# MLP products of split parts, and a second-product bank that alternates by group

## The reference, cut to what matters

```
x_norm2 = modulate(_ln(x), shift_m, scale_m)     # per sequence
h = jax.nn.gelu(x_norm2 @ W_mlp1 + b_mlp1)       # 128 -> 512 channels
h = h @ W_mlp2 + b_mlp2                          # 512 -> 128 channels
x = x + gate_m[:, None] * h
```

## Time and profile before the change

| what | value |
|---|---|
| median of three runs | 579.82 us (578.67 to 581.12) |
| profiled execution, its own time | 578.05 us |
| span of that execution (first to last instruction) | 576.3 us |
| mean granted TensorE clock | 0.994 of full |
| TensorE busy | 540.8 us (94%) |
| VectorE, ScalarE, GpSimd busy | 424.9, 385.2, 271.3 us |
| stretch of the MLP's products | 324.2 to 404.95 us |

### The profile page before, as it was taken

How to read it: one execution, slowest core, us unless ns; L and a number is a source line. 1 busy time by engine, 2 the same in 40 slices (tenths; PEclk the granted TensorE clock), 3 DMA queues, 4 the chain that set the end, 5 groups by cost and what they waited for, 6 DMA issues and landing times.

```text
span 576.3 us, 16509 instructions
## 1 busy us (share of the span) xinstructions
PE 540.8 (94%) x6175; PEld 381.4 (66%) x6177; DVE 424.9 (74%) x1255; ACT 385.2 (67%) x897; POOL 271.3 (47%) x294
## 2 busy tenths in 40 slices
PE   7988998998999999999999889988999999999995
PEld 6745665666666666666667544444788788788895
DVE  4688987878899798899787445555586786786565
ACT  6548686777878778787777744564654854854862
POOL 5638669299494878888903110124034034034000
PEclk9999999899999999999999999999999999999998
DMA  4764656254143543334400010000001001000000
GB/s 130 162 173 127 175 155 164 56 122 126 52 116 89 134 115 97 105 90 115 114 5 3 2 36 0 2 1 19 0 19 40 18 20 36 18 18 20 19 20 18
DMA packets 48716, 39.38 MB, mean 68 GB/s; under 512 B 6241, under 2 KB 48002, under 8 KB 48642
## 3 DMA queue, kind: packets, MB, share of 16 engines
q1 hardware_dynamic: 46568, 34.62, 23.1%
q10 hardware_dynamic: 2074, 3.77, 2.3%
HBM read 10.06 MB, written 2.10 MB: 21 GB/s over the span
## 4 chain that ended last, share of the span: by engine, by line
PE 64%; DVE 12%; POOL 7%; DMA 5%; SPq 4%; issue 4%; ACT 3%; ACTq 0%; DVEq 0%; POOLq 0%
PE PS L939 35%; PE PS L1810 6%; PE PS L1776 5%; DVE NM L1592 3%; PE PS L975 3%; PE PS L1862 3%; SPq L1324 3%; PE PS L1874 2%; DMA Qs<-MT 2%; PE PS L1794 2%; PE PS L1832 2%; DMA Ks<-Kp 2%; PE PS L1867 2%; POOL rstd L1370 1%; POOL rest L1401 1%
## 5 line engine op out<-in xcount | busy, mean ns | idle before, releaser
L1592 DVE TENSOR_REDUCE NM<-PS 128x4 f32<-128x512 f32 x256 | 163.3, 681 | 30.8 <-PE PS L1776 30.2
L1478 ACT ACTIVATE PR<-PS 128x512 f32<-128x512 f32 x256 | 140.0, 601 | 27.1 <-PE PS L1794 26.5
L1776 PEld LDWEIGHTS PS<-Ks,Qs 64*128 64x128 bf16 x1024 | 57.0, 94 | 53.9 <-DVE NM L1592 29.3
L1776 PE MATMUL PS<-Ks,Qs 64*128 64x128 bf16 x1024 | 83.2, 218 | 6.4 <-DVE NM L1592 3.7
L1794 PE MATMUL PS<-Qs,Ks 64*128 64x128 bf16 x1024 | 83.6, 218 | 3.8 <-DMA Qs<-MT 3.2
L1810 PE MATMUL PS<-PR,Va 128*32 128x128 f32 x2048 | 82.9, 280 | 0.0
L733 ACT ACTIVATE r_HID<-PS,ANC 128x128 f32<-128x128 f32 x224 | 63.4, 383 | 20.2 <-PE PS L939 20.2
L648 POOL TENSOR_TENSOR m_veps<-m_mv,m_eps 128x4 f32<-128x4 f32 x16 | 3.2, 201 | 143.2 <-DVE m_mv L812 143.2
L1794 PEld LDWEIGHTS PS<-Qs,Ks 64*128 64x128 bf16 x1024 | 57.0, 94 | 7.4 <-DMA Qs<-MT 3.7
L1810 PEld LDWEIGHTS PS<-PR,Va 128*32 128x32 f32 x2048 | 48.3, 109 | 20.2 <-ACT PR L1478 6.1
L939 PE MATMUL PS<-r_NXS,r_WNS 128*128 128x512 f32 x168 | 53.1, 424 | 0.0
(11 more groups left out here) (197 smaller groups left out, 1102.3 us busy)
## 6 DMA issues: line engine op xcount, KB each, us to landing
Qs<-Qp SPq DMA_DIRECT2D x96, 128.0 KB
Ks<-Kp SPq DMA_DIRECT2D x90, 128.0 KB
CTXG<-in_ctx SPq DMA_DIRECT2D x8, 256.0 KB, 3.8
r_CTX<-in_ctx SPq DMA_DIRECT2D x8, 256.0 KB, 2.7
out<-X SPq DMA_DIRECT2D x8, 256.0 KB, 2.3
X<-in_x SPq DMA_DIRECT2D x7, 256.0 KB, 4.4
W<-in_weights ACTq DMA_DIRECT2D x2, 855.0 KB
Qs<-MT SPq DMA_DIRECT2D x62, 8.0 KB
```

Source lines behind the costliest of these rows:

```text
L1478: nc.scalar.activation(PR[:, u, :], T_BANK[u % 2][:, :], ACT.Exp, scale=SCALE)\
L1592: nc.vector.tensor_reduce(out=NM[:, c.b // 2, c.second, u // 2, u % 2 * 4:u % 2 * 4 + 4, 0], in_=S_BANK[score_bank(c, u)[0]][:, :].rearran ...
L1776: last = nc.tensor.matmul(S_BANK[bank][:, j * P:(j + 1) * P], Qs[c.stack][rows, lo + j, cols], Ks[c.stack][rows, lo + j, cols], start=True ...
```

## The change

Both MLP products are computed from split parts. The weights get parts W1S and W2S, written by GpSimd in two more weight splits in round 7 (at places 9.0 and 12.0; the old ones move up in number). m_XT gets parts XTS, two buffers by the parity of the group, written by VectorE in a new step xt_parts: a copy to the high part, then a subtraction. Each chunk of m_H gets parts HS, one buffer: after its gelu ScalarE copies the chunk to the high part, and GpSimd subtracts. Every product becomes three matmuls. xt_read moves to right behind xt, and no longer waits for the firsts of the group before but for its xt_parts.

The second product's bank is PS[3] or PS[4] by parity, and the turn back goes into the same bank. So its first second(g,0) waits for x_added (turn_back of group g-2), not for gate of group g-1. The loop of cycles 3 and 4 is written out, since the parity must be known. Tiles Qs and Ks are placed elsewhere in SBUF, since the new tiles reuse freed room.

```diff
-                 + [(t, "split", "weights", k, 0) for k, t in enumerate((2.5, 6.0, 22.5, 24.5))]
+                 + [(t, "split", "weights", k, 0) for k, t in enumerate((2.5, 6.0, 9.0, 12.0, 22.5, 24.5))]
...
-                 + mlp_steps(8.46, "first", 1, 3) + mlp_steps(8.47, "xt_read", 2) + mlp_steps(8.48, "gelu", 1, 2)
+                 + mlp_steps(8.46, "first", 1, 3) + mlp_steps(8.35, "xt_read", 2) + mlp_steps(8.36, "xt_parts", 2) + mlp_steps(5.11, "xt_parts", 1) + mlp_steps(8.48, "gelu", 1, 2)
...
 MLP_STEPS = (
-    ("stats", 2, 0), ("xt", 1, 0),
+    ("stats", 2, 0), ("xt", 1, 0), ("xt_read", 1, 0), ("xt_parts", 1, 0),
     ("first", 0, 0), ("second", -1, 0), ("first", 0, 1), ("second", -1, 1),
-    ("turn_back", -2, 0), ("norm", 2, 0), ("first", 0, 2), ("first", 0, 3), ("xt_read", 1, 0),
+    ("turn_back", -2, 0), ("norm", 2, 0), ("first", 0, 2), ("first", 0, 3),
     ("second", -1, 2), ("gelu", 0, 2), ("second", -1, 3), ("gelu", 0, 3), ("gate", -1, 0),
 )
...
-    with eng.Fori(3, NG - 3) as i:
-        for name, lag, k in MLP_STEPS:
-            mlp(name, i + lag, k, 0, 0)
+    for i in range(3, NG - 3):
+        for step in valid_steps(MLP_STEPS, i):
+            mlp(*step)
...
+    W1S = rb("m_W1S", [P, 2, 4 * P], F32R)
+    W2S = rb("m_W2S", [P, 2, 4 * P], F32R)
+    XTS = [rb(f"m_XTS{k}", [P, 2, GT], F32R) for k in range(2)]
+    HS = rb("m_HS", [P, 2, 4, GT], F32R)
...
-    XT_BANK, FIRST_BANK, SECOND_BANK, BACK_BANK = PS[0], PS[1:3], PS[3], PS[4]
+    XT_BANK, FIRST_BANK, SECOND_BANK = PS[0], PS[1:3], PS[3:5]
...
+            elif name == "first" and k < 2 or name == "gelu":
+                pool.wait_ge(h_high, 4 * g + (NG + k + 1))
+                nc.gpsimd.tensor_tensor(HS[:, 1, k, :], H[:, k, :], HS[:, 0, k, :], ALU.subtract).then_inc(h_split, 1)
...
+            elif k in (2, 3):
+
+                pool.wait_ge(shifted_done, 16 * (2 * NG - 2))
+                to, source = ((W1S, w("mlp1")), (W2S, w("mlp2")))[k - 2]
+                return split(to, source, (weights_high, k + 1), weights_split)
...
             if later(g):
-                act.wait_ge(second_done, 4 * g + (k - 3))
+                act.wait_ge(h_split, 4 * g + (NG + k - 3))
             nc.scalar.activation(H[:, k, :], FIRST_BANK[k % 2][:, :], ACT.Gelu_apprx_tanh, bias=vec("bmlp1", k))\
                 .then_inc(gelu_done, 1)
+            act.wait_ge(gelu_done, 4 * g + (k + 1))
+            if later(g):
+                act.wait_ge(second_done, 4 * g + (k - 3))
+            nc.scalar.activation(HS[:, 0, k, :], H[:, k, :], ACT.Copy).then_inc(h_high, 1)
...
                 if later(g):
-                    act.wait_ge(first_done, 4 * g)
+                    act.wait_ge(xt_split, g + NG)
...
+            elif name == "xt_parts":
+                dve.wait_ge(xt_read, g + 1)
+                if g > 1:
+                    dve.wait_ge(first_done, 4 * (g - 1))
...
+                nc.vector.tensor_copy(XTS[par][:, 0, :], XT[:, :]).then_inc(xt_high, 1)
+                dve.wait_ge(xt_high, g + (NG + 1))
+                nc.vector.tensor_tensor(XTS[par][:, 1, :], XT[:, :], XTS[par][:, 0, :], ALU.subtract).then_inc(xt_split, 1)
...
-                product(FIRST_BANK[k % 2][:, :], w("mlp1", k * P, P), XT[:, :]).then_inc(first_done, 1)
+                chunk = slice(k * P, (k + 1) * P)
+                product(FIRST_BANK[k % 2][:, :], W1S[:, 0, chunk], XTS[par][:, 0, :], True, False)
+                product(FIRST_BANK[k % 2][:, :], W1S[:, 0, chunk], XTS[par][:, 1, :], False, False)
+                product(FIRST_BANK[k % 2][:, :], W1S[:, 1, chunk], XTS[par][:, 0, :], False, True).then_inc(first_done, 1)
...
-                if k == 0 and later(g):
-                    pe.wait_ge(gated, g)
-                pe.wait_ge(gelu_done, 4 * g + (k + 1))
-                product(SECOND_BANK[:, :], w("mlp2", k * P, P), H[:, k, :], start=k == 0, stop=k == 3)\
-                    .then_inc(second_done, 1)
+                if k == 0 and g > 1:
+                    pe.wait_ge(x_added, g - 1)
+                pe.wait_ge(h_split, 4 * g + (NG + k + 1))
+                chunk = slice(k * P, (k + 1) * P)
+                product(SECOND_BANK[par][:, :], W2S[:, 0, chunk], HS[:, 0, k, :], k == 0, False)
+                product(SECOND_BANK[par][:, :], W2S[:, 0, chunk], HS[:, 1, k, :], False, False)
+                product(SECOND_BANK[par][:, :], W2S[:, 1, chunk], HS[:, 0, k, :], False, k == 3).then_inc(second_done, 1)
...
                 pe.wait_ge(gated, g + 1)
-                if later(g):
-                    pe.wait_ge(x_added, g)
-                turn(BACK_BANK, lambda b: YT[0][:, b * P:(b + 1) * P]).then_inc(turned_back, 1)
+                turn(SECOND_BANK[par], lambda b: YT[0][:, b * P:(b + 1) * P]).then_inc(turned_back, 1)
...
-                    pe.wait_ge(gated, NG)
+                    pe.wait_ge(x_added, NG - 1)
```

More of the change, by code:

```diff
@@ L460, in mlp_and_router @@
 def mlp_and_router(nc, stack, X, V, ctxin, w, vec, rows1, condT, mod, gbm, half, zeros, YT, ident, PS, load_w2, out,
-                   bank_filled, bank_read, max_done, exp_done, o_normed, o_stored):
+                   bank_filled, bank_read, shifted_done, max_done, exp_done, o_normed, o_stored,
+                   high_ready, low_ready):
     def sb(name, shape, dt=F32):
@@ L555, in mlp_and_router @@
     bank_filled["mlp_xt"], bank_read["mlp_xt"] = xt_turned, xt_read
+    xt_high, xt_split, h_high, h_split = (high_ready["k0"], low_ready["k0"], high_ready["q0"], low_ready["q0"])
     masked = sem("masked")
@@ L828, in mlp @@
                 normalise(0, g, XN, xt_turned)
+            elif name == "xt_parts":
+                dve.wait_ge(xt_read, g + 1)
+                if g > 1:
+                    dve.wait_ge(first_done, 4 * (g - 1))
+                elif g == 1:
+                    dve.wait_ge(exp_done, 4 * NCORE)
+                else:
+                    dve.wait_ge(shifted_done, 16 * (2 * NG - 2))
+                nc.vector.tensor_copy(XTS[par][:, 0, :], XT[:, :]).then_inc(xt_high, 1)
+                dve.wait_ge(xt_high, g + (NG + 1))
+                nc.vector.tensor_tensor(XTS[par][:, 1, :], XT[:, :], XTS[par][:, 0, :], ALU.subtract).then_inc(xt_split, 1)
             elif name == "gate":
@@ L834, in mlp @@
                     nb = bass.ds(g * GB + b, 1)
-                    last = nc.vector.tensor_scalar(YT[0][:, b * P:(b + 1) * P], SECOND_BANK[:, b * P:(b + 1) * P],
+                    last = nc.vector.tensor_scalar(YT[0][:, b * P:(b + 1) * P], SECOND_BANK[par][:, b * P:(b + 1) * P],
                                                    mod[:, 5, nb], gbm[:, nb], ALU.mult, ALU.add)
@@ L840, in mlp @@
                 dve.wait_ge(turned_back, g + 1)
-                nc.vector.tensor_tensor(x, BACK_BANK[:, :], x, ALU.add).then_inc(x_added, 1)
+                nc.vector.tensor_tensor(x, SECOND_BANK[par][:, :], x, ALU.add).then_inc(x_added, 1)
         def router(name, g, k, par, pair):
@@ L1091, in before_router @@
         def before_router():
-            pe.wait_ge(weights_split, 2 * -(-NHC * P // GT))
+            pe.wait_ge(weights_split, 2 * -(-NHC * P // GT) + 2)
             pe.wait_ge(xt_read, NG)
@@ L1209, in build_block @@
         rest = sb("rest", [P, 2, GT])
-        Qs = [sb(f"Qs{k}", [P, NJ, GT], BF16) for k in range(STACKS)]
-        Ks = [sb(f"Ks{k}", [P, NJ, GT], BF16) for k in range(STACKS)]
         zrow = sb("zrow", [32, GT], BF16)
@@ L1221, in build_block @@
         On = sb("On", [P, 2, 2 * P])
+        Qs, Ks = [None] * STACKS, [None] * STACKS
+        for k in (1, 0, 2):
+            Qs[k], Ks[k] = (sb(f"{what}s{k}", [P, NJ, GT], BF16) for what in "QK")
         OgT = [sb(f"OgT{k}", [P, GT]) for k in range(2)]
@@ L1373, in body @@
                     extra["split"](ev[2])
+                elif ev[:2] == ("read", "mlp_xt"):
+                    extra["mlp"]("xt_parts", 0, 0, 0, 0)
                 elif ev[:2] == ("init", "third"):
```

9 lines of the change are left out of this document (5 added, 4 removed).

## The result

The changed kernel takes 587.48 us in the median of four runs (587.26 to 590.78), beside 580.47 us (578.67 to 582.96) for the kernel before: a ratio of 1.0147, with a 95% interval of 1.0096 to 1.0198. It is slower. The forecast was 573.7 us, 6.1 faster, so it has the wrong sign. Times are of executions in the chip's usual state; one of first_only_lock's ten, 582.16 us, was in a slower one and is left out.

A forecast was written before the change was run, and what follows sets the result against it. TensorE's matmuls were taken to bound the MLP, then ScalarE's chain at about 6.9 us a cycle. Milestones summed to hidden(0,0) 6.1 us earlier, so 573.7 us from 579.8, range 568 to 580.

The forecast's parts named there:

- lock term: VectorE's m_XN and xt_parts steps beside GpSimd's subtractions: waits of 0 to 5.4 us a group, put at nothing in steady cycles.
- The cover: Slack on VectorE: norm ends near 3 us into the next cycle, its turn 3 us later; without it 2 us a cycle.
- The rest of the sum: MLP terms beside the lock: product 0.68 us, ScalarE copy 0.55, GpSimd subtraction 1.27, xt_parts 1.2, cycle about 6.9.
- signs of being wrong: xt_parts above 2.5 us, copy above 0.8, cycle above 7.5, clock drop in the stalls at 373, TensorE stalled for HS before 366.
- The end: End of the MLP in GpSimd's order: last product ends 7.9 us after r_EV's copy, near 398.8; hidden(0,0) 6.1 us earlier.
- No term below is a matter of clock: Granted clock 1.00 throughout, that is 2.4 GHz, so the forecast gave the clock no cost.
- Locks eat it: Rival: six locked VectorE instructions wait 0.9 us each, on the path from cycle 3; 6 of 6 us lost, 579.8; chance 0.19.
- Slower: Rival: r_EV's copy ends after 400.0, as if ScalarE's copy took 1.0 us and cycles 8.7; 583 us; chance 0.13.
- Full gain: Rival: locks and GpSimd's order cost nothing, TensorE dense; 11.5 us of products, perhaps 2.5 of gate waits; 567 us; chance 0.12.

The follow-up runs named there:

- first_only_lock: first_only plus 32 idle GpSimd subtractions whose result no other instruction reads; 576.93 us, ratio 0.993 to before.
- halves: The changed kernel with each GpSimd subtraction of H cut into two instructions of 256 columns; 581.97 us, ratio 1.003 to before.
- no_h_low: The changed kernel with H's low part zero, so GpSimd's 32 subtractions are gone, matmuls and ScalarE's copies kept; 569.10 us, ratio 0.979 to before.
- clock_kept: The changed kernel with 38, 22 and 38 filler turns of the identity on TensorE in the three stalls; 586.45 us, ratio 1.013 to before.
- first_only: The changed kernel with only the first product split, the second float32 from H, without copies or subtractions of H; 567.77 us, ratio 0.978 to before.
- xt_early: The changed kernel with float32 MLP products and no parts, m_XT in two buffers, xt_read where the change put it; 568.91 us, ratio 0.985 to before.

## Why the prediction was wrong, point by point

**The step that failed** is the lock term: "In the steady cycles I put this at nothing: [...] norm ends near 3 us into the next even with the waits, and its turn needs it another 3 us later." The price in front of it was right. I bounded the wait at 0 to 0.9 us for each VectorE instruction; it is (4.95 - 1.11) / 4 = 0.96. The cover was wrong, and in the end of the norm, not in the place of its turn. On VectorE's queue the norm stands behind xt_parts and behind the addition of turn_back. Counted from the start a of xt_read, my own terms put xt_read's end at a+1.5, then 1.2 for xt_parts, 0.69 for the addition and 1.1 for the norm: it could not end before a+4.5 even alone, and near a+8 with 0.9 us for each step, where I wrote 3. In the trace xt_read starts at 353.26, the norm at 356.84 (a+3.6), and it ends at 361.84 (a+8.6). TensorE is ready for the turn at 361.89 - 2.94 = 358.95 (a+5.7), close to the place that I had counted. That leaves 2.1 us for a norm that takes 1.1 alone and 5.0 locked. The run with idle subtractions shows that subtractions beside VectorE cost some 9 us though nothing uses their result.

The Trainium skill (SBUF — State Buffer, "SBUF: two separate sides") lets the loser of the shared ports block for the whole of the other's instruction. The rows at 338.02 and 356.78 and the 2.79 us with halves agree with it.

**The rest of the sum held.** Split into parts, a product costs 0.68 us; the copy is 0.63 with gelus about 1.24 us apart where they follow one another; the subtraction 1.30 (4.93 / 4 = 1.23 in a row); xt_parts 0.43 + 0.69 with no lock, against my 1.2; cycles without a late norm 6.6 and 6.9. The kernel without subtractions is what my sum described in all but GpSimd, and its stretch is 71.9 us, where the forecast had 73.3 (398.8 less first(0,0) at 325.5). Of the signs of being wrong that I had named, a cycle above 7.5 us (11.4), xt_parts above 2.5 (2.8 from 380.91) and a lower clock behind a stall came; a copy above 0.8 us did not.

**Where the 18.9 us lie**, after against no_h_low: from first(0,0) to first(2,2) 24.5 against 17.0 us, from there to first(6,2) 38.4 against 30.35, and to hidden(0,0) 27.9 against 24.5. The first two pieces hold the stalls at the turns (1.30, 4.85, 2.94, 4.79). Of the 7.5 us of the first piece the lower clock makes some 2.2 (clock_kept has 22.2 there). How the rest of the other pieces divides is not shown.

**The end.** I put the last product's end 7.9 us behind r_EV's copy. r_EV was copied at 406.94 and hidden(0,0) starts at 415.43, 8.5 later: GpSimd's order there is as I read it. Only everything before it was late: keys(1) at 399.77 against a forecast of 385.5.

**The clock.** "No term below is a matter of clock" was wrong: the granted clock is 0.86 in the stages with stalls, and in the first piece of the stretch that costs 2.2 us. As the lower clock comes only behind the stalls, it is a part of what the failed step costs.

**The rivals.** "Locks eat it" had the right mechanism and "on the path from cycle 3" the right place, but its 6 us are too few: it let a lock only take back what was won, while a norm of 5 us in a gap of 2 makes the cycle longer than before. "Slower" had the right side and the right last link (r_EV later than 400.0), but named ScalarE's copy at 1.0 us as its cause, and that copy is 0.63. "Full gain" (567) adds up wrongly: 11.5 and 2.5 us are 14.0, not the 12.8 taken off. Its time was reached only by kernels without the subtractions. Of those that compute everything, first_only at 567.8 and 568.2 and xt_early at 568.9 beat both kernels.

**What I did not look for:** the gain that lay in the order. The stage before was 24.75 of 24.9 us busy, and I took that for dense. The cycle of 8.25 against 7.7 of own work stood in my own text: half a microsecond a cycle that "busy" hid, since a matmul's end is modelled.

## What to carry to other kernels

Before giving GpSimd a long SBUF operation in each cycle, list VectorE's instructions in the same stretch, stretch those that a trace shows beside GpSimd at its length (here norm and xt_parts, but not the statistics or the gate), put each behind all that the list has ahead of it on its queue, and only then compare its end with the time at which its consumer is ready in the new, shorter cycle. If the operation must stay there, cut it into shorter instructions: halves took four VectorE steps from 4.95 to 2.79 us. And compare a cycle's length with the sum of its own work, not with its busy share: here the order of one read, a second buffer and the bank brought 7.1 us of the stretch, and the cheaper first products 3.7.

## What the runs showed of the hardware that was not expected

- A VectorE operation of 0.34 us takes 1.24 us beside 1.23 us subtractions on GpSimd, 1.01 beside 1.0 us ones, and 0.70 beside 0.69 us ones: the other's length each time, within 0.01 us. VectorE's statistics (0.86 us for four) and its reads of PSUM (1.37 us) keep their time beside the same subtractions.
- GpSimd is delayed by VectorE too: the inverse deviation of 128x4 took 1.46 us at 336.59, right behind the start of the subtraction of xt_parts, and 1.01 at 379.50; before the change all nine take 1.01 to 1.02.
- The granted clock fell to 0.86 over stages with stalls of 3 to 5 us. Kept up behind the first stall, it gave 2.2 us; the later fillers took as much again, so what it costs in the whole is open.
